# Two post-norm transformer layers in one program: the gate's product in its own step, batch work dealt out anew, maxima 14 heads ahead, a weight product later

## The chip, the cores and the metric

One core of a Trainium2 chip runs the program. The metric is the device time of one execution in microseconds, and the median of several runs is compared. Less is better.

## What is computed

The input has 8 batches of 256 tokens of width 128, all in float32. Cut to what matters:

```python
# layer 0
x = layernorm(x + softmax(q k^T / sqrt(8)) v @ Wproj + bproj)          # 16 heads of size 8, bias bqkv
h = butterfly(x @ W_exp + b_exp, up_weights)                           # 512 wide, 9 stages of 2x2 mixes
x = layernorm(x + butterfly(gelu(h + up_bias), down_weights) @ W_con + b_con + down_bias)
# layer 1
q = rope(x @ Wqa @ Wqb); k, v = split(x @ Wkva @ Wkvb)                 # 4 key/value heads, each used by 4 heads
x = layernorm(x + causal_softmax(rope'd q k^T / sqrt(8)) v @ Wout + bout)
x = layernorm(x + (silu(x @ w_gate.T / 127) * (x @ w_up.T / 127)) @ w_down.T / 127)
```

## The kernel before

Each engine runs one long stream of instructions. All five streams (SP, TensorE, ScalarE, VectorE, GpSimd) are written out by the same loop over **steps**: `for g in STEPS`, where g goes up by 2, from FIRST to FINAL. There are 16 batch-layers b (8 of layer 0, then 8 of layer 1) with 16 heads each, so 256 heads in a row, and step g handles heads g and g+1. No clock ties the streams together: an engine goes through its steps as fast as its semaphore waits let it.

**Scores** (L317 `scores`). In step g TensorE computes, for heads g+LEAD and g+LEAD+1, scores into one of three banks SM (L268 `max_scores`, L282); VectorE takes each query's maximum from them (L646 in layer 0, L654 with the causal mask in layer 1). Eight heads' maxima are turned by TensorE (MT, L338), copied by ScalarE (L532) and sent by SP as an 8 KB DMA (L244) into a spare row of the stacked queries QK, so that the second score product (L286 `exp_scores`, L301, three banks ST, heads g and g+1) has the maximum subtracted. ScalarE takes the exponentials (L525). Before head 0, `filler` matmuls (L306) stand in for the second product. Four heads lie in four strips of 32 rows of the array and run side by side.

**The other work** of batch b is put at the step 16b + offset, by the constants AT_... (L44 to L49) and the helpers `batch_at`, `half_at` and `tile_at` (a tile is two batches, for layer 0's FFN). Names used below: QK, the query and key product (L388), in layer 1 followed by a swap of halves by SP (L240), the rotation on GpSimd (L799 to L801) and the copy into the strips by SP (L229); V (L402); PV, weights times values, two halves of 8 heads (L420), in layer 1 behind GpSimd's causal mask of the exponentials (L791); T, a transposition of the outcome (L345), divided on VectorE (L676 to L679); ATT, turned back (L352); PROJ, the output projection (L362) with residual and statistics on VectorE; LN, the normalisation on GpSimd (L742 `normalise`); XT, its transposition (L369). Layer 0's FFN: UP0 (L432, four), GELU (L587, one of ScalarE, with a table load before and one after), DN0 (L444, two halves), LN0, XT0 (L451). Layer 1's FFN: UP1 (L462, three chunks c, each with gate and up halves in one bank), tanh on ScalarE (L582), the product of gate and up on VectorE (L669, L671), DN1 (L471), a second LN on GpSimd (L826) and the output DMA on SP (L251).

Everything except the scores goes through two PSUM banks G, in turn. `claim` (L259) makes TensorE wait, before it uses a bank, until the claim two before it has been read out; for UP1 that is when L671 is done (semaphore `hid_ready`). In the kernel before, VectorE does L669 and L671 for the UP1 of step g in step g+2, after that step's maxima.

Within a step, TensorE does the scores first, then MT, T, ATT, PROJ, XT, QK, V, PV, UP0, DN0, XT0, UP1, DN1, and one-time work: BV (a bias product), JOIN (L480, products of layer 1's low-rank weights, which need four small loads), BXU, BXD and TURN (the butterfly weights, prepared with much work on GpSimd). Loads that aren't needed at once stand in a list `late` (L203) of 21 entries, from which SP issues one in each step from LATE on, in between its other DMAs. SP waits in order too: each of its DMAs stands behind the waits of those before.

```python
AT_QK, AT_QKIN, AT_ROPE = -36, (-34, -28), -32
AT_MT, AT_V, AT_PV = (-10, -2), -6, (10, 18)
...
        if len(claims) >= 2:
            pe.wait_ge(*claims[-2])
```

Of the kernel before, what the change touches and what calls it, by code (L numbers as in the profile page):

```python
# [6 lines left out]
NB = 8  # L7
T = 256
W = 128
P = 128  # L10
H = 16
D = W // H
# [62 lines left out]
def block_kernel(nc, x_nat, x_t, ones, wqk0, wv0, bqk0, bv0, wproj, bproj, u0, d0, fac_u, fac_d, bfw, bup, bcon, bdown,  # L75
# [7 lines left out]
    with ctx:  # L83
# [113 lines left out]
        def _(sp):  # L197
# [58 lines left out]
        def _(pe):  # L256
# [72 lines left out]
            for g in STEPS:  # L329
# [10 lines left out]
                if (b := batch_at(g, AT_T)) is not None:  # L340
# [6 lines left out]
                    ins.then_inc(A["t_ps"], 1)  # L347
                if (b := batch_at(g, AT_ATT)) is not None:
# [16 lines left out]
                if (b := batch_at(g, AT_XT)) is not None:  # L365
# [4 lines left out]
                    ins.then_inc(A["xt_ps"], 1)  # L370
                if (b := batch_at(g, AT_QK)) is not None:
# [53 lines left out]
                for c in range(HC):  # L425
                    if (n := tile_at(g, AT_UP0[c])) is not None:
                        bank = claim(("up0", n, c), F0["pre_ready"], HC * n + c + 1)
                        if c == 0:
                            pe.wait_ge(A["xt_ready"], 2 * (n + 1))
                            if n == 0:  # L430
                                pe.wait_ge(wup_ready, 1)
                        nc.tensor.matmul(bank[:, :], wup[:, c * P:(c + 1) * P], xt[:, n * FT:(n + 1) * FT],  # L432
                                         start=True, stop=True).then_inc(F0["up_ps"], 1)
                for half_tile in range(2):
                    if (n := tile_at(g, AT_DN0[half_tile])) is not None:
                        bank = claim(("dn0", n, half_tile), F0["res_done"], 2 * n + half_tile + 1)
                        if half_tile == 0:
                            pe.wait_ge(F0["hid_ready"], n + 1)
                            if n == 0:
                                pe.wait_ge(bd_out, 1)  # L440
                        for i in range(2):
                            for c in range(HC):
                                s = 2 * half_tile + i
                                ins = nc.tensor.matmul(bank[:, i * W:(i + 1) * W], hid0[:, c, s * P:(s + 1) * P], down[:, c, :],  # L444
                                                       start=(c == 0), stop=(c == HC - 1))
                        ins.then_inc(F0["down_ps"], 1)
                if (n := tile_at(g, AT_XT0)) is not None:
                    bank = claim(("xt0", n), F0["xt_ready"], n + 1)
                    pe.wait_ge(F0["ln_ready"], n + 1)
                    for s in range(FS):  # L450
                        ins = nc.tensor.transpose(bank[:, s * P:(s + 1) * P], N0["ln"][:, n % 2, s, :], id32[:, :])  # L451
                    ins.then_inc(F0["xt_ps"], 1)
                for c in range(SC):
                    if (b := batch_at(g, AT_UP1[c], (1,))) is not None:
                        i = b - NB
                        bank = claim(("up1", i, c), F1["hid_ready"], SC * i + c + 1)
                        if c == 0:
                            pe.wait_ge(A["xt_ready"], b + 1)
                            if i == 0:
                                pe.wait_ge(wf_ready, 2)  # L460
                        for s in range(2):
                            ins = nc.tensor.matmul(bank[:, s * T:(s + 1) * T], wf[:, s, c * P:(c + 1) * P],  # L462
                                                   xt[:, i * T:(i + 1) * T], start=True, stop=True)
                        ins.then_inc(F1["up_ps"], 1)
                if (b := batch_at(g, AT_DN1, (1,))) is not None:
                    i = b - NB
                    bank = claim(("dn1", i), F1["res_done"], i + 1)
                    pe.wait_ge(F1["hid_ready"], SC * (i + 1))
                    for q in range(QT):
                        for c in range(SC):  # L470
                            ins = nc.tensor.matmul(bank[:, q * W:(q + 1) * W], hid1[:, i % 2, c, q * P:(q + 1) * P],  # L471
                                                   wf[:, 2, c * W:(c + 1) * W], start=(c == 0), stop=(c == SC - 1))
                    ins.then_inc(F1["down_ps"], 1)
# [35 lines left out]
        def _(act):  # L509
# [6 lines left out]
            for g in STEPS:  # L516
# [11 lines left out]
                if (n := half_at(g, AT_MT)) is not None:  # L528
# [3 lines left out]
                    act.activation(mt[:, n % 2, :], g_bank["mt", n][0:8, 0:T], ACT.Copy).then_inc(A["mt_ready"], 1)  # L532
                if (b := batch_at(g, AT_ATT)) is not None:
# [4 lines left out]
                if (b := batch_at(g, AT_XT)) is not None:  # L538
                    act.wait_ge(A["xt_ps"], b + 1)
                    x0 = (b % NB) * T  # L540
                    act.activation(xt[:, x0:x0 + T], g_bank["xt", b][:, 0:T], ACT.Copy).then_inc(A["xt_ready"], 1)
                if (b := batch_at(g, AT_QK)) is not None:
                    act.wait_ge(A["qk_ps"], b + 1)
                    if layer(b) == 0:
# [28 lines left out]
                if (n := tile_at(g, AT_XT0)) is not None:  # L573
                    act.wait_ge(F0["xt_ps"], n + 1)
                    act.activation(xt[:, n * FT:(n + 1) * FT], g_bank["xt0", n][:, :], ACT.Copy).then_inc(F0["xt_ready"], 1)
                for c in range(SC):
                    if (b := batch_at(g, AT_UP1[c], (1,))) is not None:
                        i = SC * (b - NB) + c
                        act.wait_ge(F1["up_ps"], i + 1)
                        if i >= 2:  # L580
                            act.wait_ge(F1["hid_ready"], i - 1)
                        act.activation(th[:, i % 2, :], g_bank["up1", b - NB, c][:, 0:T], ACT.Tanh, scale=0.5)\  # L582
# [389 lines left out]
```

## Time and profile before

| | |
|---|---|
| median of 3 runs | 439.56 us (437.63 to 439.57) |
| profiled execution | 437.91 us |
| its span, first to last instruction | 436.2 us |
| busy: TensorE matmul, VectorE, ScalarE, GpSimd | 86%, 54%, 47%, 40% of the span |
| mean granted clock of TensorE | 0.927 of full speed |
| DMA | 14.04 MB, mean 32 GB/s |

All times in the rows are microseconds from the span's start, unless marked ns. PE is TensorE's matmuls, PEld its weight loads, DVE is VectorE, ACT ScalarE, POOL GpSimd, SP the queue that issues most DMAs; a q behind the name is the engine's sequencer. L with a number is the line of the kernel.
### The profile page before, as it was taken

What the parts mean: (1) busy time and instruction counts of PE and PEld (TensorE: products, weight loads), DVE (VectorE), ACT (ScalarE), POOL (GpSimd) and SP (SyncE); (2) the same over time, 40 slices, a digit from 0 to 9 for tenths busy, and PEclk for the clock granted to TensorE, in tenths of its full rate; (3) what the DMA queues carried; (4) which work ended last, traced back from release to release, by engine and by line L of the source; (5) the groups of instructions that cost most, each with busy time, mean ns of one, the idle gap of its engine ahead of it and who ended that gap; (6) DMA issues with size and microseconds to landing.
All of it is one profiled execution on the core that took longest, in us unless ns stands there. A gap on an engine that the chain in (4) does not pass through costs nothing.

```text
span 436.2 us, 10527 instructions
## 1 busy us (share of the span) xinstructions
PE 373.5 (86%) x3928; PEld 258.9 (59%) x3928; DVE 237.5 (54%) x903; ACT 203.0 (47%) x439; POOL 176.0 (40%) x298
## 2 busy tenths in 40 slices
PE   4876999999799997999797979797988979699763
PEld 2545666665477555756485647574756656477542
DVE  2462447667456664757264745565666566455232
ACT  2012566664745566564834573353353535354310
POOL 6239423020206023452147635383653626163531
PEclk9995799999989998999798997998898989999978
DMA  4862110100010101111110202011011110000000
GB/s 136 222 115 63 68 28 4 26 19 11 2 27 2 27 3 25 27 26 27 26 26 2 50 2 49 4 39 24 15 31 24 38 26 16 2 13 2 15 12 12
DMA packets 9218, 14.04 MB, mean 32 GB/s; under 512 B 2000, under 2 KB 4944, under 8 KB 9040
## 3 DMA queue, kind: packets, MB, share of 16 engines
q1 hardware_dynamic: 8736, 13.24, 13.3%
q8 instruction: 31, 0.51, 0.5%
q10 hardware_dynamic: 432, 0.13, 0.1%
q14 instruction: 19, 0.16, 0.1%
HBM read 5.76 MB, written 1.05 MB: 16 GB/s over the span
## 4 chain that ended last, share of the span: by engine, by line
PE 77%; DVE 8%; issue 5%; ACT 3%; POOL 2%; DMA 2%; SPq 2%; POOLq 0%; ACTq 0%; DVEq 0%
PE SM L282 27%; PE G L420 10%; PE ST L301 7%; PE G L462 6%; PE G L444 4%; PE G L432 4%; PE G L388 3%; PE G L362 3%; DVE masked_s L654 3%; PE G L471 3%; PE G L402 2%; PE G L338 2%; DVE hid L671 2%; DVE gated L669 1%; PE G L345 1%
## 5 line engine op out<-in xcount | busy, mean ns | idle before, releaser
L525 ACT ACTIVATE E<-ST 128x512 f32<-128x512 f32 (+1 forms) x256 | 125.5, 542 | 110.9 <-PE ST L301 110.2
L301 PE MATMUL ST<-QK 32*128 32x256 f32 (+1 forms) x1024 | 148.2, 397 | 12.3 <-ACT E L525 12.3
L282 PE MATMUL SM<-QK 31*128 31x256 f32 (+1 forms) x1024 | 152.4, 397 | 2.6 <-DMA QK<-qk 1.4
L282 PEld LDWEIGHTS SM<-QK 31*128 31x128 f32 x1024 | 102.5, 196 | 47.4 <-issue 22.0
L646 DVE TENSOR_REDUCE mx<-SM 128x2 f32<-128x512 f32 x128 | 82.4, 685 | 69.2 <-PE SM L282 69.1
L654 DVE CUSTOM_DVE_ANT_0 masked_s<-SM,mask_sb 128x256 f32<-128x256 f32 (+1 forms) x256 | 76.0, 353 | 69.6 <-PE SM L282 69.4
L301 PEld LDWEIGHTS ST<-QK 32*128 32x128 f32 x1024 | 99.4, 197 | 17.5 <-ACT E L525 15.1
L791 POOL TENSOR_SCALAR_AFFINE_SELECT E<-E 128x512 f32<-128x512 f32 x64 | 39.1, 636 | 50.4 <-ACT E L525 50.4
L420 PE MATMUL G<-E,V 128*32 128x256 f32 (+1 forms) x1024 | 56.3, 362 | 2.9 <-issue 2.3
L420 PEld LDWEIGHTS G<-E,V 128*32 128x32 f32 x1024 | 30.1, 111 | 22.6 <-issue 6.6
L743 POOL TENSOR_SCALAR nm_a<-mv_a 128x2 f32<-128x2 f32 x16 | 3.1, 191 | 99.0 <-DVE mv_a L620 99.0
L462 PE MATMUL G<-xt,wf 128*128 128x256 f32 x96 | 29.7, 442 | 11.3 <-DVE hid L671 10.0
L462 PEld LDWEIGHTS G<-xt,wf 128*128 128x128 f32 x96 | 18.2, 210 | 18.0 <-DVE hid L671 13.1
L571 ACT ACTIVATE O<-G 128x256 f32<-128x256 f32 x32 | 12.3, 383 | 32.1 <-PE G L420 32.1
L582 ACT ACTIVATE th<-G 128x256 f32<-128x256 f32 x24 | 9.2, 383 | 35.0 <-PE G L462 35.0
L669 DVE SCALAR_TENSOR_TENSOR gated<-th,G 128x256 f32<-128x256 f32 x24 | 10.0, 418 | 22.2 <-ACT th L582 22.2
L799 POOL TENSOR_TENSOR ry<-ry,ropec_sb 128x512 f32<-128x512 f32 x8 | 10.1, 1268 | 28.2 <-DMA rs<-ry 18.6
L654 DVE DVE_READ_ACCUMULATOR2_ANT mx<- 128x1 f32 x256 | 21.3, 83 | 0.0
L444 PE MATMUL G<-down,hid 128*128 128x128 f32 x128 | 19.5, 315 | 1.5 <-DVE hid L671 1.5
L444 PEld LDWEIGHTS G<-down,hid 128*128 128x128 f32 x128 | 18.3, 228 | 3.5 <-issue 1.7
L432 PE MATMUL G<-xt,wup 128*128 128x512 f32 x32 | 17.2, 618 | 0.0
L471 PE MATMUL G<-wf,hid 128*128 128x128 f32 x96 | 14.9, 316 | 1.5 <-DVE hid L671 1.5
(107 smaller groups left out, 449.7 us busy)
## 6 DMA issues: line engine op xcount, KB each, us to landing
QK<-qk SPq DMA_DIRECT2D x64, 64.0 KB
rs<-ry SPq DMA_DIRECT2D x16, 128.0 KB, 2.3
xb<-x_nat SPq DMA_DIRECT2D x1, 1024.0 KB, 9.4
out<-ln_g SPq DMA_DIRECT2D x8, 128.0 KB, 1.9
xt<-x_t SPq DMA_DIRECT2D x1, 896.0 KB, 6.2
wi<-wi_all SPq DMA_DIRECT2D x1, 576.0 KB, 3.4
QK<-mt SPq DMA_DIRECT2D x32, 8.0 KB
fac<-fac_u SPq DMA_DIRECT2D x1, 508.0 KB, 4.8
```

Of the source, the lines that this page charges most:

```text
L282: ins = nc.tensor.matmul(SM[m % S_RING][:, cols], q, QK[rows, b % QK_RING, r, 1, keys], start=True, stop=True)
L301: ins = nc.tensor.matmul(ST[m % S_RING][:, c * T:(c + 1) * T - q0], QK[rows, b % QK_RING, r, 1, c * P:(c + 1) * P], QK[rows, b % QK_RING, ...
L420: ins = nc.tensor.matmul(bank[VCOL * j:VCOL * (j + 1), q0:T], values, E[:, (2 * n + e) % E_RING, j, k * T:(k + 1) * T - q0], start=(e == 0 ...
L432: nc.tensor.matmul(bank[:, :], wup[:, c * P:(c + 1) * P], xt[:, n * FT:(n + 1) * FT], start=True, stop=True).then_inc(F0["up_ps"], 1)
L444: ins = nc.tensor.matmul(bank[:, i * W:(i + 1) * W], hid0[:, c, s * P:(s + 1) * P], down[:, c, :], start=(c == 0), stop=(c == HC - 1))
L462: ins = nc.tensor.matmul(bank[:, s * T:(s + 1) * T], wf[:, s, c * P:(c + 1) * P], xt[:, i * T:(i + 1) * T], start=True, stop=True)
L471: ins = nc.tensor.matmul(bank[:, q * W:(q + 1) * W], hid1[:, i % 2, c, q * P:(q + 1) * P], wf[:, 2, c * W:(c + 1) * W], start=(c == 0), st ...
L525: act.activation(E[:, a % E_RING, j, 0:n], ST[m % S_RING][:, 0:n], ACT.Exp, scale=SCALE)\
L646: ins = nc.vector.tensor_reduce(mx[:, n % 2, :, i], bank[:, :].rearrange("p (q k) -> p q k", q=QT), AX.X, ALU.max, negate=True)
L654: ins = nc.vector.tensor_tensor_reduce(out=masked_s[:, m % 2, lo:hi], in0=bank[:, lo:hi], in1=mask_sb[:, T + lo - hi:T], scale=-1.0, scala ...
L669: link(nc.vector.scalar_tensor_tensor(out=gated[:, i % 2, :], in0=th[:, i % 2, :], scalar=1.0, in1=bank[:, 0:T], op0=ALU.add, op1=ALU.mult))
L791: nc.gpsimd.affine_select(out=e, in_=e, pattern=[[0, 4], [1, P]], compare_op=ALU.is_ge, fill=0.0, base=0, channel_multiplier=-1).then_inc( ...
```

## The change

- UP1's product of gate and up (L669, L671) is done by VectorE in the step of its matmuls (g), not in the next; UP1 and DN1 move to other steps, ScalarE's tanh moves to just behind the maxima's copy, and the second LN gets a step of its own (AT_LN1), with the output DMA in the step after.
- LEAD is 14, not 18. QK, its copy and rotation come 4 steps' numbers earlier, MT 4 later, V 2 later; GELU, the DN0 halves, LN0, XT0 and the last UP0 chunk move too.
- TensorE's and VectorE's order inside a step: the FFN's work now stands before ATT and PROJ.
- JOIN goes from step -2 to 16, BV from -4 to 0, the late list from -30 to -20, and GpSimd's XB_AT from 8 to 10, behind the second set of butterfly paths.
- Of batch 0's four QK copies two are issued by ScalarE.

```diff
-LEAD = 18
-AT_QK, AT_QKIN, AT_ROPE = -36, (-34, -28), -32
-AT_MT, AT_V, AT_PV = (-10, -2), -6, (10, 18)
+LEAD = 14
+AT_QK, AT_QKIN, AT_ROPE = -40, (-38, -32), -36
+AT_MT, AT_V, AT_PV = (-6, 2), -4, (10, 18)
 AT_T, AT_ATT, AT_PROJ, AT_LN, AT_XT = 20, 22, 24, 26, 30
-AT_UP1, AT_DN1, AT_OUT1 = (32, 34, 36), 40, 44
+AT_UP1, AT_DN1, AT_LN1 = (32, 36, 38), 44, 50
-AT_UP0, AT_GELU, AT_DN0, AT_LN0, AT_XT0 = (48, 50, 52, 56), 58, (64, 68), 70, 76
+AT_UP0, AT_GELU, AT_DN0, AT_LN0, AT_XT0 = (48, 52, 54, 60), 64, (68, 76), 78, 80
-BXU, BXD, TURN, JOIN, BV, XB_AT, WF_AT, LATE = (4, 6), 12, 28, -2, -4, 8, 30, -30
-FIRST, FINAL = AT_QK, HEADS + 32
+BXU, BXD, TURN, JOIN, BV, XB_AT, WF_AT, LATE = (4, 6), 12, 28, 16, 0, 10, 34, -20
+FIRST, FINAL = AT_QK, HEADS + 40
...
-                        for j in range(STRIPS):
+                        for j in range(2 if b == 0 else STRIPS):
                             sp.dma_start(QK[STRIP * j:STRIP * j + ROWS, b % QK_RING, :, :, :], qk[j:P:STRIPS, b % 2, :, :])\
...
+                        if b == 0:
+                            act.wait_ge(A["qk_out"], 2)
+                            act.wait_ge(zeros_ready, 1)
+                            for j in range(2, STRIPS):
+                                act.dma_start(QK[STRIP * j:STRIP * j + ROWS, 0, :, :, :], qk[j:P:STRIPS, 0, :, :]).then_inc(qk_in[0], 16)
...
-                if (b := batch_at(g, AT_OUT1, (1,))) is not None:
+                if (b := batch_at(g - 2, AT_LN1, (1,))) is not None:
...
                 for c in range(SC):
-
-                    if (b := batch_at(g - 2, AT_UP1[c], (1,))) is not None:
+                    if (b := batch_at(g, AT_UP1[c], (1,))) is not None:
                         i = SC * (b - NB) + c
                         bank = g_bank["up1", b - NB, c]
                         dve.wait_ge(F1["th_ready"], i + 1)
...
-                if (b := batch_at(g - 2, AT_DN1, (1,))) is not None:
+                if (b := batch_at(g, AT_LN1, (1,))) is not None:
                     i = b - NB
                     pool.wait_ge(F1["var_ready"], i + 1)
```

The blocks of TensorE, ScalarE and VectorE for UP0, UP1, DN0, DN1, XT0 and PROJ are moved inside the step as told above and are otherwise the same. Order of TensorE's work in a step after: scores, MT, T, UP0, UP1, DN0, DN1, ATT, PROJ, XT, XT0, QK, V, PV, one-time work. VectorE: maxima, T, UP0, UP1, DN0, DN1, PROJ.

## Rows read from the trace of the kernel before

**Rows 1.** The page: busy time by engine, and the chain that ended last by engine

```profile
PE 373.5 (86%) x3928; PEld 258.9 (59%) x3928; DVE 237.5 (54%) x903; ACT 203.0 (47%) x439; POOL 176.0 (40%) x298
...
PE 77%; DVE 8%; issue 5%; ACT 3%; POOL 2%; DMA 2%; SPq 2%; POOLq 0%; ACTq 0%; DVEq 0%
```

**Rows 2.** TensorE's waits: waiting line, releaser, us in total, times, longest

```profile
PE ST L301 <- ACT E L525: 12.3, 6, 3.0
PE G L462 <- DVE hid L671: 10.0, 10, 1.5
PE G L352 <- DVE hid L671: 8.7, 5, 1.8
PE G L483 <- DMA wkvb_sb<-wkvb: 6.6, 1, 6.6
```

**Rows 3.** Timeline, one batch of layer 1: start, length, engine, line, idle before

```profile
319.75 0.38 ACT L582 ACTIVATE th<-G 128x256 f32<-128x256 f32 x1 [0.22 <-PE G L462]
...
321.71 0.42 DVE L669 SCALAR_TENSOR_TENSOR gated<-th,G 128x256 f32<-128x256 f32 x1
...
322.64 1.13 PE L462 MATMUL G<-xt,wf 128*128 128x256 f32 x4 [0.63 <-DVE hid L671]
...
326.70 1.13 PE L462 MATMUL G<-xt,wf 128*128 128x256 f32 x4 [1.48 <-DVE hid L671]
...
330.76 0.44 PE L352 MATMUL G<-id,at 128*128 128x128 f32 x2 [1.75 <-DVE hid L671]
```

**Rows 4.** Windows of 2 us: busy time of PE, PEld, DVE, ACT, POOL, then granted clock, DMA

```profile
46.00:48.00 2.00, 2.00 (x17) 1.20 (x18) 0.00 (x1) 0.38 (x1) 0.00 (x0) 0.50 0.00 0
...
322.00:324.00 2.00, 1.37 (x11) 0.98 (x12) 0.55 (x2) 0.57 (x2) 2.00 (x2) 1.00 0.00 0
...
332.00:334.00 2.00, 2.00 (x16) 1.78 (x9) 1.67 (x10) 0.87 (x2) 0.00 (x0) 0.50 0.03 8
```

**Rows 5.** The chain that ended last, in order of time: projections of five batches

```profile
69.18 0.64 PE G L362 x4
...
155.11 0.64 PE G L362 x4
...
250.71 0.64 PE G L362 x4
...
381.40 1.15 PE G L362 x4
...
416.01 0.72 PE G L362 x4
```

**Rows 6.** The chain in its first 56 us: start, length, what

```profile
9.92 4.50 DMA QK<-qk
...
34.06 2.16 DMA wkvb_sb<-wkvb
```

**Rows 7.** Timeline of VectorE near the start

```profile
17.15 1.29 DVE L646 TENSOR_REDUCE mx<-SM 128x2 f32<-128x512 f32 x2 [0.24 <-PE SM L282]
```

**Rows 8.** Timeline of SP near the start: the issues of DMAs

```profile
11.21 0.45 SPq L247 DMA_DIRECT2D wproj_sb<-wproj  x1
...
17.41 0.49 SPq L247 DMA_DIRECT2D d_sb<-d  x1
...
19.37 0.43 SPq L247 DMA_DIRECT2D bdown_sb<-bdown  x1
22.84 0.59 SPq L244 DMA_DIRECT2D QK<-mt  x1
```

**Rows 9.** DMA issues of 10 to 30 us: count, size, median us to landing

```profile
bdown_sb<-bdown SPq DMA_DIRECT2D x1, 64.0 KB, 8.2
```

**Rows 10.** Groups of instructions by line: busy us, mean ns, idle before

```profile
L799 POOL TENSOR_TENSOR ry<-ry,ropec_sb 128x512 f32<-128x512 f32 x8 | 10.1, 1268 | 28.2 <-DMA rs<-ry 18.6 <-issue 9.5
...
L587 ACT ACTIVATE hid<-hid 128x2048 f32<-128x2048 f32 x4 | 7.6, 1910 | 0.0
...
L587 ACT ACT_TABLE_LOAD x4 | 5.1, 1283 | 0.1
```

More of the change, by code:

```diff
@@ L347, in _ @@
                     ins.then_inc(A["t_ps"], 1)
+                for c in range(HC):
+                    if (n := tile_at(g, AT_UP0[c])) is not None:
+                        bank = claim(("up0", n, c), F0["pre_ready"], HC * n + c + 1)
+                        if c == 0:
+                            pe.wait_ge(A["xt_ready"], 2 * (n + 1))
+                            if n == 0:
+                                pe.wait_ge(wup_ready, 1)
+                        nc.tensor.matmul(bank[:, :], wup[:, c * P:(c + 1) * P], xt[:, n * FT:(n + 1) * FT],
+                                         start=True, stop=True).then_inc(F0["up_ps"], 1)
@@ new lines, in _ @@
+                for c in range(SC):
+                    if (b := batch_at(g, AT_UP1[c], (1,))) is not None:
+                        i = b - NB
+                        bank = claim(("up1", i, c), F1["hid_ready"], SC * i + c + 1)
+                        if c == 0:
+                            pe.wait_ge(A["xt_ready"], b + 1)
+                            if i == 0:
+                                pe.wait_ge(wf_ready, 2)
+                        for s in range(2):
+                            ins = nc.tensor.matmul(bank[:, s * T:(s + 1) * T], wf[:, s, c * P:(c + 1) * P],
+                                                   xt[:, i * T:(i + 1) * T], start=True, stop=True)
+                        ins.then_inc(F1["up_ps"], 1)
@@ new lines, in _ @@
+                for half_tile in range(2):
+                    if (n := tile_at(g, AT_DN0[half_tile])) is not None:
+                        bank = claim(("dn0", n, half_tile), F0["res_done"], 2 * n + half_tile + 1)
+                        if half_tile == 0:
+                            pe.wait_ge(F0["hid_ready"], n + 1)
+                            if n == 0:
+                                pe.wait_ge(bd_out, 1)
+                        for i in range(2):
+                            for c in range(HC):
+                                s = 2 * half_tile + i
+                                ins = nc.tensor.matmul(bank[:, i * W:(i + 1) * W], hid0[:, c, s * P:(s + 1) * P], down[:, c, :],
+                                                       start=(c == 0), stop=(c == HC - 1))
+                        ins.then_inc(F0["down_ps"], 1)
@@ new lines, in _ @@
+                if (b := batch_at(g, AT_DN1, (1,))) is not None:
+                    i = b - NB
+                    bank = claim(("dn1", i), F1["res_done"], i + 1)
+                    pe.wait_ge(F1["hid_ready"], SC * (i + 1))
+                    for q in range(QT):
+                        for c in range(SC):
+                            ins = nc.tensor.matmul(bank[:, q * W:(q + 1) * W], hid1[:, i % 2, c, q * P:(q + 1) * P],
+                                                   wf[:, 2, c * W:(c + 1) * W], start=(c == 0), stop=(c == SC - 1))
+                    ins.then_inc(F1["down_ps"], 1)
@@ L370, in _ @@
                     ins.then_inc(A["xt_ps"], 1)
+                if (n := tile_at(g, AT_XT0)) is not None:
+                    bank = claim(("xt0", n), F0["xt_ready"], n + 1)
+                    pe.wait_ge(F0["ln_ready"], n + 1)
+                    for s in range(FS):
+                        ins = nc.tensor.transpose(bank[:, s * P:(s + 1) * P], N0["ln"][:, n % 2, s, :], id32[:, :])
+                    ins.then_inc(F0["xt_ps"], 1)
                 if (b := batch_at(g, AT_QK)) is not None:
@@ L423, in _ @@
                     ins.then_inc(A["pv_ps"], 1)
[L425 to L473, printed above, removed]
@@ L532, in _ @@
                     act.activation(mt[:, n % 2, :], g_bank["mt", n][0:8, 0:T], ACT.Copy).then_inc(A["mt_ready"], 1)
+                for c in range(SC):
+                    if (b := batch_at(g, AT_UP1[c], (1,))) is not None:
+                        i = SC * (b - NB) + c
+                        act.wait_ge(F1["up_ps"], i + 1)
+                        if i >= 2:
+                            act.wait_ge(F1["hid_ready"], i - 1)
+                        act.activation(th[:, i % 2, :], g_bank["up1", b - NB, c][:, 0:T], ACT.Tanh, scale=0.5)\
+                            .then_inc(F1["th_ready"], 1)
                 if (b := batch_at(g, AT_ATT)) is not None:
@@ L541, in _ @@
                     act.activation(xt[:, x0:x0 + T], g_bank["xt", b][:, 0:T], ACT.Copy).then_inc(A["xt_ready"], 1)
+                if (n := tile_at(g, AT_XT0)) is not None:
+                    act.wait_ge(F0["xt_ps"], n + 1)
+                    act.activation(xt[:, n * FT:(n + 1) * FT], g_bank["xt0", n][:, :], ACT.Copy).then_inc(F0["xt_ready"], 1)
                 if (b := batch_at(g, AT_QK)) is not None:
@@ L571, in _ @@
                     act.activation(O[:, b % 2, t, :], g_bank["pv", n][:, 0:T], ACT.Copy).then_inc(A["o_ready"], 1)
[L573 to L582, printed above, removed]
-                            .then_inc(F1["th_ready"], 1)
                 if (n := tile_at(g, AT_GELU)) is not None:
```

63 lines of the change are left out of this document (32 added, 31 removed).

## The prediction

> **What bounds the kernel now.** I read the chain of waits first: TensorE carries 77% of it, ScalarE 3% and GpSimd 2% [rows 1]. So a step costs what its matmuls cost, and an edit pays only if TensorE stops waiting or runs faster. Then the waits of TensorE [rows 2]: 12.3 us on ScalarE's exponentials, 10.0 and 8.7 us on VectorE's gate product at L671, 6.6 us on a weight load at L483. The timeline shows the gate product's waits inside one batch of layer 1 [rows 3]: the gate of the matmuls issued in step g is multiplied by VectorE one step later, behind that step's maxima, and the G bank it holds is claimed two claims on. TensorE stands 0.63 us, 1.48 us and 1.75 us in turn, 3.86 us a batch, in five batches (those whose UP1 steps lie beside full steps): 19.3 us. The windows show a second loss [rows 4]: behind that 1.75 us, at 332 us, TensorE was granted 0.50, its level of 1.2 GHz, although busy throughout, and behind the 6.6 us at L483 the same at 46 us. The chain in order of time gives milestones, the projection of each batch (L362) [rows 5]: batches 0, 4, 8, 13 and 15 start it at 69.18, 155.11, 250.71, 381.40 and 416.01 us. I go from one to the next. From 416.01 to the end of the span are 20.2 us.
>
> **The start, to batch 0's projection.** At L483 TensorE stops until wkvb is there, issued at 34.06 and landed 2.16 us later [rows 6]; its SP instruction stands behind other waits. JOIN at step 16 takes this wait away. Its matmuls, 0.76 us and about as much again, half of that at full speed, stay on the path, with BV's small one, now in step 0: +1.1 us. The late list's own issue moves from step -30 to -20, past batch 1's QK copy on SP. What is late next is the row of maxima of the first eight heads (SP L244), which the first exponential needs. Scores ahead of it go at 1.53 us a step (two maxima of 1.29 us together, and 0.24 us idle) [rows 7]; seven such steps from about 13.1 us (the copy of rows 6 landed at 14.42 and comes 1.3 us sooner, below), with QK(2), MT and V between, bring TensorE to step 0 at about 26 us. But the row is an 8 KB transfer behind all bulk loads. Before, it was issued at 22.84 us, behind bdown, issued at 19.37 [rows 8], which took 8.2 us to land [rows 9], so at 27.6 us; the first load, wproj, went out at 11.21 us [rows 8]. Now the first load goes out when batch 1's copy is through, at 17.41 us [rows 8], 6.2 us later; batch 2's copy stands ahead of the row in place of batch 1's, and bup, bcon and bdown, some 1 us, behind it. So it lands at about 27.6 + 6.2 - 1.3 = 32.5 us. Bounds: 27 us, if only SP's own issues count (25.0 us plus the 2.16 us of wkvb), and 34 us. I take 32.5, as the load just ahead of it in the queue is the nearest row [rows 9]. Step 0 of before had its exponentials' scores when JOIN was through, 2 us behind wkvb, at 38.3 us: -5.8 us. TensorE again idles 6.5 us, so I take the same slow stretch after it. JOIN's wait is replaced more than removed. Term: -5.8 + 1.1 = **-4.7 us** (bounds -16 and 0).
>
> Half of batch 0's QK copy now goes out on ScalarE's queue. The last of SP's four issues began at 9.92 us and landed 4.50 us later [rows 6]; two issues fewer save 1.3 us, and at most as much could come of it. It pulls forward steps that then wait for the row of maxima anyway: 0. The Trainium skill, DMA: Bandwidth & Descriptors, section Issuing engines are not separate DMA queues, says that SP's and ScalarE's DMAs share the same 16 DMA engines and that only issue time is saved. By that alone nothing faster than 1.3 us could come of it, and the sum stays as it is; no row before shows a copy split so.
>
> **LEAD 14 for 18.** 137 steps with scores become 135: two steps of filler and maxima less, two with exponentials alone less, two full ones more. The first two lie in the wait just priced; TensorE's score work is the same, and a step of exponentials alone is held by ScalarE, so 0 (at most -3). The row of maxima now has two steps instead of four to reach its consumer, over 4 us against some 3 of copy, issue and landing: 0, with rope or mask waits on SP not ahead of it.
>
> **Layer 0.** MT leaves steps 6 and 14 for 2 and 10, QK goes from 12 to 8, V from 10 to 12. Steps 0, 6 and 14 get light, and a step can't be shorter than the 1.53 us of VectorE's two maxima: batches 0 to 2 **+0.8 us**, half a step of waiting. From batch 2 the FFN fills just these steps. The GELU costs 1.91 us and two table loads of 1.28 us [rows 10], 4.5 us in which no exponential goes. Before, GELU followed step 10's PV, and TensorE waited about 3.0 us each of four times [rows 2]; now it comes right behind step 0's exponentials, while TensorE still has the scores and PV of step 2, about 3.3 us: some 2.7 us. DN0's second half moves from step 4 to 12, at the same price. Batches 2 to 4 -0.9, 4 to 6 -0.5 (-0.3 a GELU, the rest from steps better filled). Batches 6 to 8: an early wait at PV for GpSimd's mask goes (-3), but LN0 of tile 2 now stands behind the rotation, three passes of 1.27 us [rows 10], and XT0 waits for it: +2.7. Together **-1.7 us**.
>
> **Layer 1, batches 8 to 13** (130.7 us). Gate in its own step. The claims after it find their bank free except two: PV in step 2 (tanh 0.38, two products of 0.42 us each [rows 3], reached by TensorE about 0.3 us too early) and PROJ in step 8, about as much. VectorE now stands at the gate for tanh, some 0.35 us, and behind it are queued the next two maxima, for which TensorE's scores wait two steps later. By then TensorE has issued at least one other matmul group of 1.1 us in steps 2, 4 and 6, so the ring of three SM banks covers this. If that cover went, each gate would cost its whole chain. I take 0.9 us a batch for all of it (bounds 0.3, and 3.5 as much as now): -19.3 + 4.5. The slow stretches: five beyond those at a GELU, each about 3.4 us long by windows like the one at 332 us [rows 4], half of which is lost, 1.6 us. Nothing left is longer than the 0.63 us before 322.64 us, around which the clock stayed at 1.00 [rows 3, 4]: -8.0. MT in step 2 and 10 issues its DMA past no wait. Mask, rotation and LN stand on GpSimd in another order: the mask of heads 12 to 15 comes after 3.8 us of rotation, ready about 0.6 us before PV wants it; the second LN, now in step 2, leaves LN's step. Term: **-22.8 us**, bounds -27 and -6.
>
> **The end.** The last LN_g stands no longer ahead of the last mask (it comes after it in the program now), but TensorE is then held by XT and UP1: -0.6; one short slow stretch -0.3; last batch unchanged: **-0.9 us**.
>
> **Sum**: -4.7 + 0.8 - 1.7 - 22.8 - 0.9 = -29.3 us. The profiled execution took 437.91 us with its span of 436.2; so 408.6 us. The median of the runs shown is 1.65 us above it: 410.3 us, which I give.
>
> **The rivals.** (a) *The row of maxima isn't late.* The transfers don't queue in the order of issue; it lands at 27 us, TensorE idles 1 us and never drops to its slow level. For: copies issued late overlap bulk loads. Against: bdown's 8.2 us. Another 11 us off: 399 us. Chance 0.13.
> (b) *A new wait in layer 1.* GpSimd's rotation, 3.8 us, now between the mask of step 12 and that of step 0, holds PV in step 2. GpSimd is busy 40% of the span [rows 1] and has room, but only 0.6 us at this place. Should the swap's DMA be 2 us later than I place it, PV waits 1.5 us and the clock's loss stays: five batches by 3.1 us, 426 us; half of it, 418 us. Chance 0.18.
> (c) *Slower: the gate stalls the maxima.* VectorE at its gate waits for TensorE, ScalarE, then two products and the first maximum, 0.38 + 0.42 + 0.42 + 0.7 = about 2 us, and TensorE stands as long at each of 24 gates: 48 us instead of 4.5, so 454 us. It decides once VectorE reaches the maxima of step g+2 later than TensorE the scores of step g+4; by my count it is at least 1 us from there. Chance 0.04.
> (d) *The gate's waits were a symptom.* Another engine's limit comes out at 24.7 us a batch as before, only the start gains: 434 us. VectorE's 54% of the span [rows 1] speak against it. Chance 0.04.
>
> **Numbers.** Forecast 0.61. The range of the forecast alone is 403 to 417; to hold 8 in 10 it takes in (a) and most of (b): 400 to 424. A measurement of this kernel can tell about 0.5%, 2.2 us, from no change: faster 0.94, same 0.02, slower 0.04.
>
> **What would show it.** Waits of TensorE on L671 at or near nothing except at PV and PROJ, below 0.5 us each; granted clock 1.00 through layer 1 but for the GELU; projections of layer 1 20 to 21 us apart. A wait of ST at the first exponential for the DMA from mt until 32.5 us, then a slow stretch to about 46; batch 0's projection at 64.5. GELU waits of 2.7 us. I am wrong if the L301 or L282 waits on VectorE grow past 5 us, if PV waits for the mask in every batch, or if the start gains 15 us or nothing.

## The result and the profile after

The changed kernel takes 405.62 us (median of 4 runs, 402.57 to 407.04) against 438.60 us for the kernel before on the same chip: ratio 0.924, 95% interval 0.918 to 0.930, so 33 us less. The forecast was 410.3 us, with a range of 400 to 424. The profiled execution of the changed kernel took 402.57 us with a span of 400.8; its mean granted clock is 0.962 instead of 0.927. Some executions of one and the same kernel run at a lower granted clock and take some per cent longer; ratios are of the undisturbed ones.

The page of the kernel after, busy time by engine and the chain by engine, beside [rows 1]:

```profile
PE 357.8 (89%) x3912; PEld 245.6 (61%) x3912; DVE 238.6 (60%) x903; ACT 204.9 (51%) x439; POOL 176.2 (44%) x298
...
PE 68%; POOL 10%; DVE 8%; issue 6%; ACT 5%; DMA 2%; SPq 1%; POOLq 0%; DVEq 0%; ACTq 0%
```

The other engines do the same work as before, to within 2 us. TensorE's busy time is 16 us shorter with nearly the same matmuls (3912 for 3928), which is nearly all clock. The rest of the gain, 20 us of span, is idle time. TensorE's waits after, largest first, beside [rows 2]:

```profile
PE ST L302 <- DMA QK<-mt: 7.2, 1, 7.2
PE ST L302 <- ACT E L526: 6.9, 4, 2.0
PE G L419 <- POOL ln_f L752: 4.5, 4, 2.8
...
PE G L406 <- DVE hid L694: 2.6, 7, 0.7
...
PE G L470 <- DVE hid L694: 1.1, 5, 0.2
PE SM L283 <- DVE mx L652: 1.0, 3, 0.3
PE G L470 <- POOL E L796: 0.7, 1, 0.7
...
PE SM L283 <- DVE mx L660: 0.2, 1, 0.2
```

Lines have moved: L302 and L283 are the scores for exponentials and maxima, L652 and L660 the maxima of layer 0 and of layer 1, L406 PROJ, L470 PV, L419 XT0 (which waits for LN0, `ln_f`), L694 the gate product. The 18.7 us on the product at UP1 and ATT are gone but for 0.2 us. What is left of it in layer 1's full batches stands at PROJ and PV. The wait for wkvb is gone too, and in its place stands one of 7.2 us for the row of maxima. The chain in order of time gives the same milestones as [rows 5], batches 0, 4, 8, 12, 13 and 15:

```profile
63.68 0.64 PE G L406 x4
...
148.53 0.64 PE G L406 x4
...
243.64 0.69 PE G L406 x4
...
330.38 0.71 PE G L406 x4
348.75 0.71 PE G L406 x4
...
381.85 0.73 PE G L406 x4
```

From one to the next: the start -5.5 us (63.68 against 69.18), batches 0 to 4 -1.1, 4 to 8 -0.5, 8 to 13 -25.6, 13 to 15 -1.5, the end -1.2. Sum -35.4 us of span. So nearly three quarters came out of five batches of layer 1. Windows over exactly this stretch, first of the kernel before, then after (columns as in [rows 4]: busy time of each engine from PE on, and at the end granted clock, DMA share and GB/s):

```profile
250.71:381.40 130.69, 108.25 (x1224) 80.39 (x1223) 75.16 (x416) 58.96 (x138) 63.48 (x111) 0.91 0.10 22
```

```profile
243.64:348.75 105.11, 98.93 (x1223) 74.45 (x1223) 75.42 (x417) 59.16 (x139) 63.22 (x111) 0.98 0.14 28
```

The same 1223 matmuls are busy 9.3 us less (clock 0.91 to 0.98), and TensorE idles 6.2 us (105.11 - 98.93) where it idled 22.4: 16.3 us less. From batch 9's projection (268.68 us) on, the granted clock is 1.00 in each of the four stretches from projection to projection; two of them take 19.2 us. The stretch from batch 8's projection to batch 9's is another matter: layer 0's last GELU lies in it, the clock is 0.93, and it went from 32.10 to 25.04 us.

The timeline of TensorE in one full batch shows its two waits on a product; [rows 3] had 0.63, 1.48 and 1.75 us:

```profile
330.38 0.71 PE L406 MATMUL G<-wout_sb,att 128*128 128x128 f32 x4 [0.30 <-DVE hid L694]
...
341.61 1.51 PE L470 MATMUL G<-E,V 128*32 128x256 f32 x32 [0.21 <-DVE hid L694]
```

The start, in the chain:

```profile
25.47 8.64 DMA QK<-mt
34.16 0.80 PE ST L302 x2
```

The 8 KB row of maxima leaves at 25.47 us and lands at 34.1, and TensorE resumes at 34.16. Windows around it:

```profile
28.00:30.00 2.00, 0.00 (x0) 0.00 (x0) 0.00 (x0) 0.00 (x0) 0.64 (x1) 0.80 1.08 117
30.00:32.00 2.00, 0.00 (x0) 0.00 (x0) 0.00 (x0) 0.00 (x0) 0.00 (x0) 0.50 1.04 98
...
36.00:38.00 2.00, 2.00 (x16) 1.47 (x18) 1.02 (x3) 1.08 (x2) 1.92 (x3) 0.50 0.00 0
38.00:40.00 2.00, 2.00 (x20) 0.90 (x16) 1.00 (x2) 0.92 (x2) 1.92 (x4) 0.64 0.00 0
```

TensorE stands, and its clock falls to the lower level of 1.2 GHz while it stands, at about 29.2 us. The clock stays there when TensorE works again without a pause, and is back at full speed at about 39.4 us (both times worked out from the mean clock of the windows, 0.80 and 0.64). The DMA engines are busy in the two windows from 28 to 32 us (shares of 1.08 and 1.04), though they move only 117 and 98 GB/s.

### The profile page after: what moved, and what is told of

It is laid out like the page before. It is cut to its first block, busy times and chain, and to the rows that moved or that the text cites. A ratio compares the mean times of both kernels' runs of the same rounds, so it can differ in the third digit from the quotient of the medians.

```text
span 400.8 us, 10496 instructions
## 1 busy us (share of the span) xinstructions
PE 357.8 (89%) x3912; PEld 245.6 (61%) x3912; DVE 238.6 (60%) x903; ACT 204.9 (51%) x439; POOL 176.2 (44%) x298
## 4 chain that ended last, share of the span: by engine, by line
PE 68%; POOL 10%; DVE 8%; issue 6%; ACT 5%; DMA 2%; SPq 1%; POOLq 0%; DVEq 0%; ACTq 0%
PE SM L283 22%; PE G L470 11%; PE ST L302 6%; PE G L367 5%; PE G L380 4%; PE G L356 3%; PE G L438 3%; PE G L406 2%; PE G L389 2%; PE G L346 2%; DMA QK<-mt 2%; POOL ln_f L752 2%; POOL QK L787 2%; PE G L339 2%; DVE gated L692 2%
## 5 line engine op out<-in xcount | busy, mean ns | idle before, releaser
L302 PE MATMUL ST<-QK 32*128 32x256 f32 (+1 forms) x1024 | 138.6, 380 | 14.2 <-DMA QK<-mt 7.2
L283 PE MATMUL SM<-QK 31*128 31x256 f32 (+1 forms) x1024 | 148.7, 381 | 1.2 <-DVE mx L652 1.0
L283 PEld LDWEIGHTS SM<-QK 31*128 31x128 f32 x1024 | 98.9, 186 | 40.5 <-issue 20.1
L652 DVE TENSOR_REDUCE mx<-SM 128x2 f32<-128x512 f32 x128 | 82.5, 687 | 67.7 <-PE SM L283 67.7
L302 PEld LDWEIGHTS ST<-QK 32*128 32x128 f32 x1024 | 93.1, 187 | 18.4 <-ACT E L526 8.9
L660 DVE CUSTOM_DVE_ANT_0 masked_s<-SM,mask_sb 128x256 f32<-128x256 f32 (+1 forms) x256 | 76.0, 353 | 42.5 <-PE SM L283 42.0
L470 PE MATMUL G<-E,V 128*32 128x256 f32 (+1 forms) x1024 | 55.6, 358 | 1.8 <-DVE hid L694 1.1
L470 PEld LDWEIGHTS G<-E,V 128*32 128x32 f32 x1024 | 29.7, 110 | 23.4 <-issue 7.3
L367 PE MATMUL G<-xt,wf 128*128 128x256 f32 x96 | 27.9, 420 | 1.6 <-ACT xt L550 1.5
L660 DVE DVE_READ_ACCUMULATOR2_ANT mx<- 128x1 f32 x256 | 21.2, 83 | 0.0
L380 PE MATMUL G<-down,hid 128*128 128x128 f32 x128 | 19.6, 317 | 0.0
L540 ACT ACTIVATE th<-G 128x256 f32<-128x256 f32 x24 | 9.2, 384 | 13.7 <-PE G L367 13.1
L562 ACT ACTIVATE qk<-G,bqk_sb 128x256 f32<-128x256 f32 x16 | 6.7, 471 | 17.2 <-PE G L438 17.2
L752 POOL TENSOR_SCALAR ln_a<-r_a,nm_a,rstd_a 128x128 f32<-128x128 f32 x32 | 14.2, 452 | 1.8
```

The costliest lines, as they stand in the source:

```text
L283: ins = nc.tensor.matmul(SM[m % S_RING][:, cols], q, QK[rows, b % QK_RING, r, 1, keys], start=True, stop=True)
L302: ins = nc.tensor.matmul(ST[m % S_RING][:, c * T:(c + 1) * T - q0], QK[rows, b % QK_RING, r, 1, c * P:(c + 1) * P], QK[rows, b % QK_RING, ...
L470: ins = nc.tensor.matmul(bank[VCOL * j:VCOL * (j + 1), q0:T], values, E[:, (2 * n + e) % E_RING, j, k * T:(k + 1) * T - q0], start=(e == 0 ...
L652: ins = nc.vector.tensor_reduce(mx[:, n % 2, :, i], bank[:, :].rearrange("p (q k) -> p q k", q=QT), AX.X, ALU.max, negate=True)
L660: ins = nc.vector.tensor_tensor_reduce(out=masked_s[:, m % 2, lo:hi], in0=bank[:, lo:hi], in1=mask_sb[:, T + lo - hi:T], scale=-1.0, scala ...
L752: ins = nc.gpsimd.tensor_scalar(N["ln"][:, parity, s, :], N["r"][:, s, :], N["nm"][:, s:s + 1], N["rstd"][:, s:s + 1], ALU.add, ALU.mult)
```

## The experiments

Ratios are to the kernel before on the same chip. The first four ran on one chip, where the kernel before took 434.0 us (median); the next four on one where it took 433.2; the last four on one where it took 436.6. Only on the last did the change itself run beside them.

**Gate alone.** The kernel before, with VectorE's gate in step g, and T's division moved ahead of it:

```diff
+                if (b := batch_at(g, AT_T)) is not None:
...
-                    if (b := batch_at(g - 2, AT_UP1[c], (1,))) is not None:
+                    if (b := batch_at(g, AT_UP1[c], (1,))) is not None:
```

> The kernel before with one edit: VectorE multiplies the gate (L669, L671) in the step of its matmuls, behind T's division; every other step number stays. Theory A (the gate's lateness alone held the G banks): TensorE's waits on the product fall from 23 us in all to under 5, the slow stretches of the clock at 301, 308, 332, 356 and 380 us go, batches 8 to 13 take about 109 us between projections instead of 130.7, and the time is 416 us. Theory B (the waits go only where UP1 stands in steps spread apart, since VectorE at its gate delays the maxima): half of the waits come back as waits of TensorE on VectorE's maxima, and the time is 427 us or more.

416.8 us, ratio 0.9605 (0.957 to 0.964), as the first theory had it. Its waits of TensorE on the product:

```profile
PE G L471 <- DVE hid L680: 1.5, 1, 1.5
...
PE G L352 <- DVE hid L680: 1.2, 4, 0.3
PE G L362 <- DVE hid L680: 1.2, 1, 1.2
PE G L462 <- DVE hid L680: 0.9, 1, 0.9
```

and the window from batch 8 to batch 13:

```profile
249.04:359.07 110.03, 102.68 (x1223) 77.06 (x1223) 74.19 (x417) 58.51 (x138) 63.38 (x111) 0.97 0.12 26
```

This one edit takes 20.7 us out of these five batches (130.69 to 110.03): 15.1 us of idle time (22.4 to 7.35) and 5.6 us of busy time, with the clock at 0.97. The start is as before (projection 0 at 69.09). The full change takes 4.9 us more out of the five batches, and all of that from batch 8's projection to batch 9's: 25.04 us there, against 31.03 here and 32.10 before. In the other four batches this one edit alone gains 19.6 us and the full change 18.5.

**Gate back.** The changed kernel, with only the product a step later again:

```diff
-                    if (b := batch_at(g, AT_UP1[c], (1,))) is not None:
+                    if (b := batch_at(g - 2, AT_UP1[c], (1,))) is not None:
```

> The kernel after with one edit undone: the gate's product again one step after its matmuls (g - 2). Theory A: TensorE waits for it at PV in step 2 (about 1.9 us), at ATT in step 6 (1.0) and at PROJ in step 8 (2.1), 5 us a batch in five or six batches, and the clock falls again once a batch: 27 + 8 us on top of 405.6, so about 438 us. Theory B (the new steps give most of the gain): 411 us, waits on the product under 8 us in all.

436.4 us, ratio 1.006 (1.003 to 1.009), near the first theory's 438. Its waits:

```profile
PE G L406 <- DVE hid L694: 11.4, 7, 2.1
PE G L470 <- DVE hid L694: 7.2, 5, 1.8
...
PE G L396 <- DVE hid L694: 4.2, 5, 1.0
```

The three lines are 22.8 us of waits on one product, and with single waits at three other lines 28.7. A full batch of layer 1 takes 23.75 us, and the whole gain of the change is gone. By itself the gate's step brings half of the gain, and without it none is left.

**JOIN alone.** The kernel before with `JOIN` 16 for -2.

> The kernel before with JOIN at step 16 instead of -2, nothing else. In this kernel the row of maxima is in at 27.6 us, before TensorE comes to step 0 at about 30.5 us. Theory A: no stop at all at the start, the 6.6 us and the slow stretch of 34.7 to 48.4 us both go, JOIN's matmuls cost 0.8 us later: -13 us, 425 us. Theory B: another wait takes JOIN's place, as in the kernel after: -5 us, 433 us.

421.1 us, ratio 0.973 (0.969 to 0.977): 12.9 us, where the first theory had 13. Batch 0's projection starts at 57.20 us, 12 us earlier. Windows of 2 us show TensorE busy 1.74 us or more in each from 20 to 48 us, at a granted clock of 1.00. In layer 1 it waits as before (10.0 and 8.7 us on the product). So the wait for wkvb was worth 12 us, and the full change took only 5.5 of them.

**LEAD alone.** The kernel before with

```diff
-LEAD = 18
+LEAD = 14
...
-AT_MT, AT_V, AT_PV = (-10, -2), -6, (10, 18)
+AT_MT, AT_V, AT_PV = (-6, 2), -6, (10, 18)
```

> The kernel before with LEAD 14 and MT at (-6, 2), nothing else. Theory A: two steps less are worth nothing where the start is held by loads and the end by exponentials: 437 us, within 2 us of before. Theory B: each step with scores less is worth its 1.5 to 2.5 us: 433 us. A third outcome: the row of maxima, now with two steps to its consumer, is late in each half batch: over 445 us.

447.1 us, ratio 1.034 (1.026 to 1.041): 13 us slower. The third outcome had such a time, but for another reason: TensorE waits for the row of maxima only 1.6 us in all. Its waits:

```profile
PE G L483 <- DMA wkvb_sb<-wkvb: 8.5, 1, 8.5
PE G L420 <- ACT mt L532: 7.5, 13, 0.7
```

and one of the thirteen waits on `mt` in the timeline:

```profile
71.88 1.93 PE L420 MATMUL G<-E,V 128*32 128x256 f32 x32 [0.66 <-ACT mt L532]
```

MT at -6 now stands in one step with V and PV, and PV, the third claim of the step, comes back to MT's bank, which ScalarE has yet to copy. That is the gate's own fault in small: a bank claimed before its reader is through. The change moves V to -4 as well, and this wait is absent from it. What LEAD by itself is worth isn't separated by this run.

The gate alone and JOIN alone give -17.3 and -12.9 us. If the two gains add up (they did not run together), that is a ratio of 0.931 to 0.933. The whole change gave 0.924 and, repeated below, 0.927, each within 0.006. So all the other moves together bring a few us at most: they gain 4.9 us in layer 1, and at the start the change gets 5.5 us where JOIN alone gets 12.

**Late list earlier.** The changed kernel with `LATE` -30 for -20, so that the loads leave before batch 1's copy.

> The kernel after with the late list from step -30 again (LATE -30 for -20), so that the bulk loads go out 6 us sooner and the row of maxima finds a shorter queue. Theory A (the row lands behind all loads issued before it, in the order of issue): it lands at about 28.5 us instead of 34.1, TensorE waits 1.5 us instead of 7.2, the slow stretch after it goes, and the time falls by 7 us or more, to about 398. Theory B (the row's 8.6 us come from something else, such as the strided copy of batch 2 right ahead of it): it stays at 33 us or later and the time within 2 us of the kernel after.

403.7 us, ratio 0.928 (0.921 to 0.936), no gain against the change's 0.924 and 0.927. Row and wait, in the chain and in the waits:

```profile
25.75 6.49 DMA QK<-mt
```

```profile
PE ST L302 <- DMA QK<-mt: 5.9, 2, 5.0
```

The row still took 6.5 us and landed at 32.2, and TensorE waited 5.0 us for it, so the loads issued ahead of it are not all: by the theory that blamed them alone it was to land at 28.5. What also stood ahead of the row was batch 2's strided copy. The windows of this run:

```profile
28.00:30.00 2.00, 0.00 (x0) 0.00 (x0) 0.00 (x0) 0.00 (x0) 1.31 (x5) 0.89 0.68 81
30.00:32.00 2.00, 0.00 (x0) 0.00 (x0) 0.00 (x0) 0.00 (x0) 1.92 (x3) 0.50 0.38 48
```

Twelve late loads are issued by 21.8 us, and the last of them has landed at 28.3. Then come the copy, from 22.02 us on, one weight load (wout) at 25.26 and the row at 25.75, and behind the row four small weight loads, from 26.37 to 28.6. While TensorE stands, the DMA engines move only 81 and 48 GB/s. The first of the loads behind the row, wqa with 32 KB, took 3.0 us and so landed at 29.4, before the row: it isn't the order of issue alone that decides. The copy's share in the row's 6.5 us isn't told apart from that of the weight loads by this run.

**Row by ScalarE.** The changed kernel; the first row is issued by ScalarE behind its own copy, not by SP behind batch 2's:

```diff
+                    if n == 0:
+                        act.wait_ge(A["mt_ready"], 1)
+                        act.dma_start(QK[MAXROW:P:STRIP, 0, 0:2, 0, :], mt[:, 0, :]).then_inc(m_in[0], 16)
```

> The kernel after with the first row of maxima (8 KB) issued by ScalarE, right behind its copy, instead of by SP; all else the same. Theory A: what holds the row is SP's place in line and the loads queued ahead of it in SP's own queue, so from the other queue it lands before 27 us, TensorE has no wait at step 0 and stays at full clock; the butterfly weights (BXD) may now be late by up to 3 us: 398 us. Theory B: the 16 DMA engines are the shared line whatever the queue, and the row still lands at 31 us or later: 404 us.

398.5 us, ratio 0.917 (0.911 to 0.924).

```profile
22.40 6.73 DMA QK<-mt
```

It left 3.1 us earlier, while SP was still issuing batch 2's copy (21.47 to 24.26 us), and still needed 6.7 us. Both theories missed: it landed at 29.1, between their 27 and 31, and the time was that of the first. TensorE waits 2.4 us in place of 7.2, the windows show the lower clock for some 6.8 us only, between 28 and 36 us, and projection 0 starts at 59.03. Against the version without the split copy (below, same chip, 0.925 to 0.939) that is 6.6 us, and the intervals don't meet (just: 0.924 and 0.925).

**XT0 later.** The changed kernel with `AT_XT0` 84 for 80.

> The kernel after with XT0 at step 84 instead of 80 (it must come before step 88's QK of layer 1). Theory A: LN0 is merely too slow for a step 80, so the waits of TensorE at XT0 (4.5 us in four, the longest 2.8) go, with one slow stretch: -5 us, 400.5. Theory B: what is late next, PV's mask behind LN0 or QK's input, takes half of it: -2 us.

408.4 us (404.73 to 413.8), ratio 0.943 (0.934 to 0.953): no gain of 2 or 5 us, rather a loss, though the change did not run on this chip. XT0's wait on LN0 goes, and another comes. In the waits, and at its longest in the timeline:

```profile
PE G L470 <- POOL E L796: 6.6, 2, 4.1
...
PE G L419 <- DVE at L671: 2.1, 4, 0.6
```

```profile
236.10 2.63 PE L470 MATMUL G<-E,V 128*32 128x256 f32 x32 [4.09 <-POOL E L796]
```

PV now waits for GpSimd's mask. GpSimd's work at this place is merely waited for one consumer later. Moving the consumer mends nothing; its own order would have to change, which wasn't tried.

**Copy not split.** The changed kernel with all four of QK(0)'s copies on SP (`range(STRIPS)`, ScalarE's two issues left out).

> The kernel after with all four of batch 0's QK copies issued by SP, as before. Theory A: the first scores start up to 1.3 us later, but step 0 still waits for the row of maxima at 34 us: no difference, within 1 us. Theory B: SP's queue is also shorter by two issues, so the row itself comes sooner with the split: undoing it costs 1.3 us or more.

405.1 us, ratio 0.932 (0.925 to 0.939). No difference from the change, on two other chips, can be told; 1.3 us would be less than such a comparison shows. The chain settles it better:

```profile
25.57 7.58 DMA QK<-mt
```

Without the split the row leaves at 25.57 us, with it at 25.47 and 25.67, so the shorter queue does not send it sooner. The lower clock lasts from about 28 to 45 us here, behind a wait of 6.1 us.

**The change once more**, on the chip of the last three:

> The kernel after, unchanged, as the measure for the other three on this chip: 405 us, 0.93 of the kernel before. The length of the slow stretch behind step 0's wait was 10.24 us in its first profile and 13.65 and 17.07 us in two sister kernels; it may come out anywhere among these.

404.4 us, ratio 0.927 (0.921 to 0.933). Wait for the row 7.4 us, lower clock behind it for 10.2 us, projection 0 at 64.13, layer 1 at 19.23 us a batch (311.65 to 330.88).

**A slower gate.** The changed kernel with two more products of 128x256 behind each of the 24 gates, on a tile of their own, 0.85 us of VectorE's time (two of 424 ns, the median in the trace):

```diff
+                        for _ in range(2):
+                            link(nc.vector.tensor_tensor(spare[:, 0, :], spare[:, 1, :], spare[:, 1, :], ALU.mult))
```

> The kernel after, with two more products of 128x256 on VectorE (0.9 us together, on a tile of their own) behind each of the 24 gates, after the product that frees the bank. It measures how far rival (c) is away. Theory A (VectorE at the gate is at least 1 us ahead of the scores that need its maxima): TensorE gets no new waits on the maxima, the time stays within 2 us of the kernel after. Theory B (the margin is used up): most of 24 x 0.9 = 21 us shows, as waits of TensorE on the maxima or on later products: 415 us or more.

411.4 us, ratio 0.942 (0.935 to 0.949): 7 us more than the change beside it, between the two theories. The wait on layer 1's maxima (here L662), and the longest waits of a full batch of layer 1 in the timeline:

```profile
PE SM L284 <- DVE mx L662: 0.2, 1, 0.2
```

```profile
317.51 0.71 PE L407 MATMUL G<-wout_sb,att 128*128 128x128 f32 x4 [0.32 <-DVE hid L696]
...
329.75 1.51 PE L471 MATMUL G<-E,V 128*32 128x256 f32 x32 [0.36 <-POOL E L800]
```

The maxima still aren't waited for any longer than in the change (0.2 us in all). A batch takes 20.27 us instead of 19.23: 1.04 us for some 2.5 us more work. PV now waits for the mask, the place of rival (b). In the profiled executions, which lie 10.5 us apart, 2.9 are the start, where the clock stayed low until about 47 us instead of 40.

**The row ahead of the copy.** The changed kernel; the copies of layer 0's batches go out 4 steps' numbers later each, so that batch 2's stands behind the row on the same queue, and the late list is earlier:

```diff
-AT_QK, AT_QKIN, AT_ROPE = -40, (-38, -32), -36
+AT_QK, AT_QKIN, AT_ROPE = -40, (-34, -32), -36
...
-BXU, ..., LATE = (4, 6), 12, 28, 16, 0, 10, 34, -20
+BXU, ..., LATE = (4, 6), 12, 28, 16, 0, 10, 34, -30
```

> The kernel after with LATE -30 and layer 0's QK copies two steps later each (AT_QKIN -34 for -38), so that SP issues batch 2's copy behind the first row of maxima instead of ahead of it; both rows go on SP. Theory A (the copy of 256 KB in 2 KB pieces at 50 to 100 GB/s was what kept the row back in the run with the early list): the row lands at 28 us, TensorE waits about 1 us and the clock stays up: 7 to 8 us below the kernel after. Theory B (bulk loads hold it as long): it lands at 31 us or later and the gain is under 3 us.

394.89, 393.93 and 398.97 us, ratio 0.907 (0.899 to 0.915): some 8 us faster than the change on the same chip (0.921 to 0.933), and the fastest version here. From the run with the late list earlier (0.921 to 0.936, another chip) it differs in the copies' steps alone, and the intervals don't meet. The mean granted clock of the three was 0.972, 0.974 and 0.962. The profiled execution was a fourth, of 544.59 us at a clock of 0.562, so where the row lands in an execution at full clock isn't shown. In this one it left at 28.26 us, ahead of batch 2's copy at 29.52. The DMA engines moved nothing from 28 to 29 us and 8 GB/s from 29 to 30, about 8 KB and as much as the row, and TensorE began its exponentials' scores at 33.37 us without a wait for it. There the row took at most 5.1 us, but the bulk loads were through when it left.

**Both.** The same, with the row issued by ScalarE as above.

> As the run before, and the first row issued by ScalarE. Theory A: with the copy out of the way and the bulk loads nearly through, the other queue saves at most the rest of the wait: 9 us below the kernel after, no wait of ST on the row. Theory B: no more than the run before, since both queues share the DMA engines.

400.5 us, ratio 0.916 (0.909 to 0.923): not better than the row by ScalarE alone (0.911 to 0.924), and 3.9 us below the change where the first theory had 9: the gains didn't add up. SP's and ScalarE's queues in the timeline:

```profile
22.87 2.63 SPq L230 DMA_DIRECT2D QK<-qk  x4
...
23.60 0.59 ACTq L536 DMA_DIRECT2D QK<-mt  x1
```

SP no longer waits for the row, so it sends batch 2's copy at 22.87 us, before ScalarE issues the row at 23.60. The row then takes 6.5 us, as in the two runs (late list earlier, row by ScalarE) where that copy was issued ahead of it or around it. This fits the account that the order on one queue had helped in the run before, and that taking the row off that queue undid it. The times alone don't show that it was undone: the intervals (0.899 to 0.915 and 0.909 to 0.923) overlap, and this profile is of the slowest of the four executions, 404.54 us.

## Why the prediction was right, and where its sizes were off

**What bounds the kernel**: right. TensorE's waits on one product, issued a step late on VectorE, and the clock that fell behind them were the loss of layer 1. Undoing that one line costs the whole gain, and doing it alone (with T's division moved ahead of it) brings 0.9605, half of the gain.

**Layer 1**, -22.8 us forecast, -25.6 measured. The mechanism was right: the gate's edit alone brought -20.7 us. The closeness of the rest is in part luck. The forecast spread its gain evenly over five batches. The change gained 18.5 us in the last four, and 7.1 us from batch 8's projection to batch 9's, of which the gate alone gives 1.1. The remaining 6 us there come from the other moves, which the term put at nothing but for their new waits. Which of them it was isn't shown; the wait at the GELU in this stretch, 2.96 us before and with the gate alone, is 1.97 us after. In the sum, two sizes were off by little each. The new waits at PV and PROJ were put at 0.9 us a batch and measured 0.21 + 0.30 = 0.5; idle time fell by 16.3 us instead of 14.8 (19.3 - 4.5). The clock gave back 9.3 us of busy time instead of 8.0. A full batch takes 19.23 us, below the 20 to 21 that were to be seen.

**The start**, -4.7 us forecast, -5.5 measured, from two errors that nearly cancel. The row left at 25.47 us (25.0 forecast), but landed at 34.1, not 32.5, at the upper bound of 34: the working took bdown's landing for the row's and gave batch 2's copy no more than its issues, and the runs speak for a price of its own: loads sent earlier left the row at 6.5 us, and with the copy behind the row the kernel was some 8 us faster. How the 8.6 us divide between loads and copy isn't shown. Exponentials' scores came 4.1 us sooner (34.16 against 38.3), the first exponential 3.75, where 5.8 stood. On the other side the lower clock lasted until 39.4 us, not 46: 10.2 us of it where the kernel before had 13.7. No experiment gives a reason for that, so here the sum came out by luck. "JOIN's wait is replaced more than removed" held: JOIN alone gives 12 us, JOIN with the rest of the change 5.5.

The split copy, put at 0, gives no difference that can be told. The Trainium skill, DMA: Bandwidth & Descriptors, section Issuing engines are not separate DMA queues, says that DMAs issued by SP and by ScalarE share the same 16 DMA engines. The traces agree as far as they go: the row still took 6.7 us from ScalarE's queue, and the split did not send it sooner.

**LEAD**, put at 0 (at most -3): not shown by itself. The run meant for it met a wait for MT's bank instead, which the prediction had not looked for.

**Layer 0**, +0.8 and -0.9 to batch 4, -0.8 from 4 to 8: measured -1.1 and -0.5. The half step of waiting in batches 0 to 2 was too dear (+0.2 measured for +0.8). GELU waits are 2.0 us at most, not 2.7, and batches 2 to 4 gave -1.2 for -0.9. Batches 4 to 8 came out near by two misses: 4 to 6 lost 0.7 where -0.5 stood, for a reason that isn't shown, and 6 to 8 gave -1.2 where -0.3 stood. The wait at PV that was counted off at 3 us was one of 2.3 us in the kernel before (until 233.44 us), and is gone. XT0's wait for the second LN behind the rotation came out as worked out: the chain shows the three passes and the LN,

```profile
226.21 1.24 POOL ry L804
227.44 1.23 POOL rs L805
...
228.75 1.27 POOL qk L806
...
231.66 1.76 POOL ln_f L752 x4
...
233.56 0.69 PE G L419 x4
```

and the wait at L419 is 2.8 us (2.7 forecast). **The end** gave -2.7 us, where -0.9 stood. These sizes and layer 1's make the forecast 6 us of span too high (-29.3 against -35.4); the median lies 3.05 us above the profiled run instead of 1.65, and so 4.7 us remain.

**The rivals.** (a), the row not late, fell: 7.2 us of waiting. (b), PV held by the mask in every batch of layer 1, is not there, but near: it shows once, 0.73 us at 284.77 us, behind XT0's last wait; XT0 later calls up the wait of 4.1 us in tile 2, and 0.85 us more at each gate makes it show at 0.34 and 0.36 us in full batches of layer 1. (c), the gate stalls the maxima, fell; the margin of "at least 1 us" stood up to a test with 0.85 us. (d), a symptom, fell with the first two experiments.

**Open**: why the lower clock at the start lasts 7 to 17 us with waits that differ little (7.2 us before 10.2 us of it in the change; 7.3 us before some 17 in the slower gate, and 6.1 us before some 17 with the copy not split); how much of the row's time is the loads' and how much the copy's; where the row lands in the fastest version; what LEAD alone is worth; which move gained the 6 us between the projections of batches 8 and 9; and GpSimd's order of LN0, rotation and mask.

## What to carry to other kernels

In a pipeline written out by hand, ask for every buffer how many claims away the next one is, and whether its reader has run by then; one consumer one step late cost 18.7 us of waits at two places here and the clock behind them, and moving it back was one line and the order of one block. Behind a removed wait look for the transfer that is late next, and count what stands ahead of it on its queue and on the DMA engines. The fastest version here sent the small row that TensorE waits for before a copy that nobody waited for yet. When a change moves many things, run its one or two main edits alone: here the gains of two add up to nearly the whole, and the rest had a loss at the start to mend.

## What the hardware showed unexpectedly

- A transfer of 8 KB took 8.6 us behind loads and a copy (7.6 to 9.1 us in five other runs with it at this place), and 6.5 to 6.7 us from another engine's queue. The other queue did not let it pass. Later in a run such a row took 2.8 us (slower gate, at 92.45 us).
- Behind batch 2's copy within SBUF and one weight load, with four small loads issued behind it, the row waited while the DMA engines moved 81 and 48 GB/s (late list earlier), where they reach 372 and 386 GB/s in the windows of the change from 22 to 26 us.
- After a wait of only 2.4 us at the start, the clock was at the lower level for 6.8 us in the row by ScalarE, and after one of 2.2 us for 13.7 us in the slowest execution of the run of both, TensorE busy in nearly all of it.
